# A perceiver block on one core: row statistics by group on GpSimd, one stream for two small attention layers, feed-forward and query projections interleaved

## The reference

```python
def _layernorm(x, axis=-1, eps=1e-05):
    m = jnp.mean(x, axis=axis, keepdims=True)
    v = jnp.var(x, axis=axis, keepdims=True)
    return (x - m) / jnp.sqrt(v + eps)
...
x = x + _L0_xattn_ref(_layernorm(x, axis=-1), ctx_1024, ctx_1024, ...)
x = x + _L0_attn_ref(_layernorm(x, axis=-1), ...)
x = x + _L0_ffn_ref(_layernorm(x, axis=-1), L0_ffn_weight, L0_ffn_weight_scale, L0_ffn_bias)
x = x + _L1_xattn_ref(_layernorm(x, axis=-1), ctx_1024, ctx_1024, mask_Bx1xSxS2_bf0, ...)
x = x + _L1_attn_ref(_layernorm(x, axis=-1), ...)
x = x + _L1_ffn_ref(_layernorm(x, axis=-1), ...)
```

## Time and profile before

| What | us |
|---|---|
| median of 3 runs (1117.49 to 1120.31) | 1117.58 |
| the profiled execution's own time | 1111.67 |
| its span | 1109.9 |
| busy: PE / DVE / ACT / POOL | 975.9 / 685.6 / 420.7 / 313.3 |
| first normalised tile | 24.64 |
| last tile of the second small layer normalised | 268.71 |
| first tile of the feed-forward normalised | 303.45 |
| first matmul of the cross attention's tiles | 378.03 |

### The profile page before, as it was taken

How to read it: one execution, slowest core, us unless ns; L and a number is a source line. 1 busy time by engine, 2 the same in 40 slices (tenths; PEclk the granted TensorE clock), 3 DMA queues, 4 the chain that set the end, 5 groups by cost and what they waited for, 6 DMA issues and landing times.

```text
span 1109.9 us, 40433 instructions
## 1 busy us (share of the span) xinstructions
PE 975.9 (88%) x16761; PEld 748.0 (67%) x16790; DVE 685.6 (62%) x1843; ACT 420.7 (38%) x1066; POOL 313.3 (28%) x328
## 2 busy tenths in 40 slices
PE   1899888998625899999999999999698979999999
PEld 0777656777412588888888888887477656666656
DVE  4678667887697366666666666666564633444436
ACT  1222223322253465655555565554433212222211
POOL 3101201110076234433333334431223024444430
PEclk9999888999856999999999999999697899999999
DMA  6000400000001011121111111110282011111116
GB/s 220 22 22 25 149 4 2 4 4 4 2 1 45 1 47 47 51 78 55 47 47 46 48 46 47 46 47 3 86 345 77 0 34 59 61 61 59 57 43 227
DMA packets 29743, 63.04 MB, mean 57 GB/s; under 512 B 5872, under 2 KB 22320, under 8 KB 26128
## 3 DMA queue, kind: packets, MB, share of 16 engines
q1 hardware_dynamic: 25840, 50.41, 13.0%
q0 software_dynamic: 3744, 10.23, 2.9%
HBM read 51.32 MB, written 9.31 MB: 55 GB/s over the span
## 4 chain that ended last, share of the span: by engine, by line
PE 57%; issue 5%; ACT 3%; DVE 3%; DVEq 0%; ACTq 0%; PEldq 0%
PE psum L722 13%; PE psum L1433 7%; PE psum L1441 6%; PE psum L795 6%; PE psum L784 4%; PE psum L810 3%; PE psum L1309 3%; ACT x_p L878 2%; PE psum L1088 2%; PE psum L1425 2%; PE psum L643 1%; PE psum L1329 1%; PE psum L765 1%; PE psum L1319 1%; PE psum L1194 1%
## 5 line engine op out<-in xcount | busy, mean ns | idle before, releaser
L878 ACT ACTIVATE x_p<-x_s,x_nmax 128x257 f32<-128x257 f32 x256 | 127.4, 499 | 112.0 <-DVE x_nmax L911 112.0
L941 DVE COPY x_pT<-psum 128x512 f32<-128x512 f32 x128 | 88.2, 689 | 67.7 <-PE psum L795 65.3
L911 DVE CUSTOM_DVE_ANT_0 x_s<-psum,x_mask 128x257 f32<-128x257 f32 x256 | 93.6, 423 | 44.3 <-PE psum L784 43.9
L795 PE MATMUL psum<-ident,x_p 128*128 128x128 f32 x512 | 80.0, 279 | 8.3 <-ACT x_p L878 1.7
L1433 PE MATMUL psum<-me_w,me_in 128*128 x156 | 77.1, 616 | 5.1 <-ACT me_in L1453 0.7
L1441 PEld LDWEIGHTS psum<-me_w,me_out 128*128 128x128 f32 x312 | 59.2, 190 | 25.3 <-issue 19.3
L1441 PE MATMUL psum<-me_w,me_out 128*128 x312 | 73.8, 379 | 0.9 <-DVE me_out L1488 0.9
L795 PEld LDWEIGHTS psum<-ident,x_p 128*128 128x128 f32 x512 | 58.2, 141 | 20.0 <-ACT x_p L878 18.3
L968 POOL TENSOR_TENSOR x_ctx1l<-x_ctx,x_ctx1h 128x2128 fp32r<-128x2128 f32 x8 | 37.9, 4743 | 113.6 <-ACT x_ctx1h L649 113.6
L1460 ACT ACTIVATE me_sh<-me_sb 128x512 f32<-128x512 f32 x39 | 24.5, 629 | 117.1 <-DVE me_sb L1474 117.1
L810 PEld LDWEIGHTS psum<-x_v,x_pT 128*32 128x32 f32 x4096 | 44.8, 112 | 32.8 <-DVE x_pT L941 20.1
(11 more groups left out here) (275 smaller groups left out, 2497.8 us busy)
## 6 DMA issues: line engine op xcount, KB each, us to landing
x_ctx<-in_ctx SPq DMA_DIRECT2D x16, 1064.0 KB, 4.9
me_w<-in_moe_w SPq DMA_DIRECT2D x8, 1024.0 KB, 12.4
me_got<-moe_outs SPq DMA_DIRECT2D x8, 512.0 KB, 8.2
x_mask<-in_mask SPq DMA_DIRECT2D x16, 128.5 KB, 3.7
x<-in_x SPq DMA_DIRECT2D x4, 512.0 KB, 5.5
sm_cT<-in_ctx SPq DMA_DIRECT2D x16, 128.0 KB, 2.1
me_eb<-in_moe_eb SPq DMA_DIRECT2D x1, 2048.0 KB, 24.6
moe_rows<-me_xn SPq DMA_DIRECT2D x4, 512.0 KB, 3.4
```

Source lines behind the costliest of these rows:

```text
L795: mm = nc.tensor.transpose(psum[:, 6, (2 * r + k) * P:(2 * r + k + 1) * P], x1_p[:, column(b, CB * c + r), k * P:(k + 1) * P], ident[:])
L878: nc.scalar.activation(x1_p[:, n, :], x1_s[:, rg, :], ACT.Exp, bias=x1_nmax[:, par, n:n + 1], scale=-1.0, accum_out=x1_sum[:, par, n:n + 1 ...
L911: nc.vector.tensor_tensor_reduce(out=x1_s[:, rg, :], in0=psum[:, 2 + rg, 0:SK], in1=x1_mask[par][:, b, :], scale=1.0, scalar=-2 * MASKED, ...
L941: nc.vector.tensor_copy(x1_pT[:, c].rearrange("p r k s -> p (r k s)"), psum[:, 6, :]).then_inc(x1["pT_ready"], 1)
```

## The change

Four things are changed. (1) For the first four layers the statistics are made per group of four tiles by GpSimd (`pool_rstd`: 15 operations of 128x4, one of them a power of -0.5, in 11 links that wait for one another), and no engine waits for more than its group (`group_ready`). The last two layers keep the old way. (2) The two small layers are one stream of 32 tiles; the bias product of the second layer is made in the fifth tile's last stages, its split bias after tile 8, the 8-bit weights at tile 15, the split weights of the cross attention after tile 20. (3) The feed-forward rounds and the query groups alternate: round i, then the queries of group i - 1, on TensorE and on ScalarE, which now normalises for the queries too and which takes turned tiles in pairs. (4) The first context is split after the last query normalisation, and GpSimd adds the cross attention's output bias to a tile of `x` within the tile loop.

```diff
+        layers = ["mix1", "moe1"]
+        early_layers = ["xattn0", "attn0", "ffn0", "xattn1"]
+        ln_ready, ln_step = sem("ln_ready"), sem("ln_step")
+        ln_work = sb("ln_work", [P, 6, U])
+        ln_power = sb("ln_power", [P, U])
+        ln_shift = sb("ln_shift", [P, NT])
+        ln_steps = [0]
+        ln_groups = [0]
+        def group_ready(eng, layer, g):
+            eng.wait_ge(ln_ready, early_layers.index(layer) * (NT // U) + g + 1)
+        def pool_rstd(pool, stats, count, g):
+            def done(*ins):
+                for i in ins:
+                    i.then_inc(ln_step, 1)
+                ln_steps[0] += len(ins)
+                pool.wait_ge(ln_step, ln_steps[0])
+            own = slice(g * U, (g + 1) * U)
+            mean, rstd = ln_mv[:, own, 0], ln_rstd[:, own]
+            diff, both, spread, var, root, power = (ln_work[:, n, :] for n in range(6))
+            pool.wait_ge(stats, count)
+            if ln_groups[0] > 0:
+                pool.wait_ge(ln_ready, ln_groups[0])
+            ln_groups[0] += 1
+            done(nc.gpsimd.tensor_tensor(diff, bn_out[:, own, 1], bn_out[:, own, 4], ALU.subtract),
+                 nc.gpsimd.tensor_tensor(both, bn_out[:, own, 1], bn_out[:, own, 4], ALU.add),
+                 nc.gpsimd.tensor_tensor(spread, bn_out[:, own, 2], bn_out[:, own, 5], ALU.add))
+            done(nc.gpsimd.tensor_scalar(mean, both, 0.5, None, ALU.mult),
+                 nc.gpsimd.tensor_tensor(diff, diff, diff, ALU.mult),
+                 nc.gpsimd.tensor_scalar(spread, spread, 1.0 / D, EPS, ALU.mult, ALU.add))
+            done(nc.gpsimd.tensor_scalar(diff, diff, 0.25, None, ALU.mult))
+            done(nc.gpsimd.tensor_tensor(var, spread, diff, ALU.add))
+            done(nc.gpsimd.tensor_tensor(root, var, ln_power[:], ALU.pow))
+            done(nc.gpsimd.tensor_tensor(power, root, root, ALU.mult))
+            done(nc.gpsimd.tensor_tensor(power, power, var, ALU.mult))
+            done(nc.gpsimd.tensor_scalar(power, power, -0.5, 1.5, ALU.mult, ALU.add))
+            done(nc.gpsimd.tensor_tensor(rstd, root, power, ALU.mult))
+            done(nc.gpsimd.tensor_tensor(both, mean, rstd, ALU.mult))
+            nc.gpsimd.tensor_scalar(ln_shift[:, own], both, -1.0, None, ALU.mult).then_inc(ln_ready, 1)
...
-            for s in range(NT + depth):
-                step(lambda d: (s - d, (s - d) % U), lambda d: 0 <= s - d < NT)
+            for s in range(len(smalls) * NT + depth):
+                step(lambda d: (s - d, (s - d) % U), lambda d: 0 <= s - d < len(smalls) * NT)
...
+                    if t == U:
+                        bias_product(smalls[1])
+                    if t in (0, U):
+                        pe.wait_ge(smalls[t // U].bias_ready, 1)
...
-            act_sqrt(act, c.name)
+        def small_scalar(act):
             nc.scalar.preload_act_table(ACT.Exp)
-            first = c.before
             act.wait_ge(sm_zeroed, 2)
-            act.wait_ge(sm["shift_ready"], smalls.index(c) + 1)
...
+                    if u == 0:
+                        group_ready(act, layer(t).name, t % NT // U)
+                    r = t % NT
+                    nc.scalar.activation(sm_xn[:, u, :], x[:, r, :], ACT.Identity, bias=ln_shift[:, r:r + 1],
+                                         scale=ln_rstd[:, r:r + 1]).then_inc(sm["norm_ready"], 1)
...
-            dve_rstd(dve, c.name)
-            nc.vector.scalar_tensor_tensor(out=sm_shift[:], in0=ln_mv[:, :, 0], scalar=-1.0, in1=ln_rstd[:], op0=ALU.mult,
-                                           op1=ALU.mult).then_inc(sm["shift_ready"], 1)
...
+                if live(0) and n(0)[0] == NT - 1:
+                    ffn_weights(dve)
...
+        def small_pool(pool):
+            for g in range(NT // U):
+                pool_rstd(pool, x_stats, U * (g + 1), g)
+                if g == 0:
+                    small_bias(pool, smalls[0])
+            for t in range(len(smalls) * NT):
+                r, c = t % NT, layer(t)
+                if r == 0:
+                    pool.wait_ge(c.bias_ready, 1)
+                pool.wait_ge(sm["norm_ready"], t + 1)
+                nc.gpsimd.tensor_tensor(x[:, r, :], x[:, r, :], c.b_o[:], ALU.add).then_inc(sm["x_biased"], 1)
+                if t == 8:
+                    small_bias(pool, smalls[1])
+                if t >= 10 and t % U == 2 and (t - 10) // U < NT // U + 2:
+                    g = (t - 10) // U
+                    pool_rstd(pool, sm["stats_ready"], U * (g + 1), g % (NT // U))
+                if t == 20:
+                    x1_pool_weights(pool)
...
+            dve.wait_ge(x1["weights_loaded"], 16 * 8)
+            dve.wait_ge(x1["bias_product"], 1)
+            nc.vector.tensor_tensor(x1_bo[:], psum[:, 6, 0:D], x1_bo[:], ALU.add).then_inc(x1["bias_ready"], 1)
...
+                if i == 0:
+                    pool_rstd(pool, sm["stats_ready"], NT + 3 * U, 2)
                 for u in range(U):
                     pool.wait_ge(f8["magic_ready"], U * i + u + 1)
                     v = f8_xn[:, i % 2, u, :]
                     nc.gpsimd.tensor_tensor(v, v, f8_magic[:, u, :], ALU.add).then_inc(f8["added"], 1)
+                if i == 0:
+                    pool_rstd(pool, sm["stats_ready"], NT + 4 * U, 3)
+                if i > 0:
+                    pool_rstd(pool, f8["stats_ready"], U * i, i - 1)
+            pool_rstd(pool, f8["stats_ready"], NT, ROUNDS - 1)
...
+                for v in range(PAIRS):
+                    act.wait_ge(f8["qT_done"], U * i + 2 * v + 2)
+                    if i > 0:
+                        act.wait_ge(f8["out_done"], U * (i - 1) + 2 * v + 2)
+                    nc.scalar.activation(f8_qT[:, 2 * v:2 * v + 2, :, :].rearrange("p u k s -> p (u k s)"),
+                                         psum[:, v, :].bitcast(BF16)[:, 0:2 * D], ACT.Copy).then_inc(f8["qT_ready"], 2)
+                if i > 0:
+                    queries_scalar(act, i - 1)
+            group_ready(act, "ffn0", ROUNDS - 1)
+            for k in range(KC):
+                context_high(act, 0, 0, k)
+            mask(act, 0, 0)
+            queries_scalar(act, ROUNDS - 1)
...
+        def queries_tensor(pe, i):
+            for v in range(PAIRS):
+                pe.wait_ge(x1["norm_ready"], U * i + 2 * v + 2)
+                if i > 0:
+                    pe.wait_ge(x1["xT_ready"], PAIRS * (i - 1) + v + 1)
+                for n in range(2):
                     for k in range(KC):
+                        mm = nc.tensor.transpose(psum[:, 4 + v, (n * KC + k) * P:(n * KC + k + 1) * P],
+                                                 x1_xn[:, 2 * v + n, k * P:(k + 1) * P], ident[:])
+                mm.then_inc(x1["xT_done"], 1)
+            pe.wait_ge(x1["xT_ready"], PAIRS * (i + 1))
+            if i == 0:
+                pe.wait_ge(x1["bias_ready"], 1)
+            for m in range(KC):
+                if i > 0:
+                    pe.wait_ge(x1["q_ready"], KC * (i - 1) + m + 1)
+                for k in range(KC):
+                    mm = nc.tensor.matmul(psum[:, 6 + m, :], x1_wq[:, k, m * P:(m + 1) * P], x1_xT[:, k, :],
+                                          start=(k == 0), stop=(k == KC - 1))
+                mm.then_inc(x1["q_done"], 1)
+        def queries_scalar(act, i):
+            group_ready(act, "xattn1", i)
+            if i > 0:
+                act.wait_ge(x1["xT_done"], PAIRS * i)
+            for u in range(U):
+                t = U * i + u
+                nc.scalar.activation(x1_xn[:, u, :], x[:, t, :], ACT.Identity, bias=ln_shift[:, t:t + 1],
+                                     scale=ln_rstd[:, t:t + 1]).then_inc(x1["norm_ready"], 1)
+            if i == 0:
+                group_ready(act, "ffn0", ROUNDS - 1)
+            else:
+                act.wait_ge(x1["q_done"], KC * i)
+            for v in range(PAIRS):
+                act.wait_ge(x1["xT_done"], PAIRS * i + v + 1)
+                nc.scalar.activation(x1_xT[:, :, v * 2 * P:(v + 1) * 2 * P].rearrange("p k (u s) -> p k u s", u=2),
+                                     psum[:, 4 + v, :].rearrange("p (u k s) -> p k u s", u=2, k=KC), ACT.Copy).then_inc(x1["xT_ready"], 1)
+            for m in range(KC):
+                act.wait_ge(x1["q_done"], KC * i + m + 1)
+                nc.scalar.activation(x1_qT[:, m, i * U * P:(i + 1) * U * P], psum[:, 6 + m, :], ACT.Identity,
+                                     bias=x1_bq[:, m:m + 1]).then_inc(x1["q_ready"], 1)
...
+            small_tensor(pe)
+            x1_bias_product(pe)
+            for i in range(ROUNDS):
+                ffn_tensor(pe, i)
+                if i > 0:
+                    queries_tensor(pe, i - 1)
+            queries_tensor(pe, ROUNDS - 1)
...
+            nc.gpsimd.memset(x1_plT[:], 0.0).then_inc(x1["zeroed"], 1)
+            pool.wait_ge(x1["bias_ready"], 1)
+            pool.wait_ge(x1["norm_ready"], NT)
+            x1_context(pool, 0, 0)
...
```

(2 more changed lines are left out.)

300 lines of the change are left out of this document (118 added, 182 removed).

## The result

The changed kernel took 1086.67 us (median of 4 runs, 1083.43 to 1088.43) against 1118.94 (1117.49 to 1121.35) of the kernel before, measured beside it: ratio 0.9706, 95% interval 0.9675 to 0.9737, 32.3 us less. Measured again it took 1087.74 against 1117.91, ratio 0.9742 (0.9696 to 0.9789), 30.2 less. The forecast was 22.8 less.

A forecast was written before the change was run, and what follows sets the result against it. TensorE was busy 88% of the span, with VectorE bounding the feed-forward. Start 7.7, boundary 13.2, feed-forward and queries 1.9 made 22.8 us less, taken from the median 1117.58: 1094.8 us, own range 1088 to 1101, 8 in 10 1083 to 1110.

The forecast's parts named there:

- Start: Up to the first normalisation: GpSimd's first group replaces the wait for VectorE's shift and 8-bit weights; 7.7 us less.
- R: Time of one group of statistics on GpSimd: 15 operations and 10 handovers, 4.2 us, between 2.5 and 17.7.
- Boundary: Between the two small layers: one stream removes 19.3 us of drain, statistics, table loads and refilling; 13.2 left after costs.
- The bias product: Second small layer's bias product: TensorE and VectorE wait for each other once; costs 1.9 us.
- Feed-forward and queries: From ScalarE free to the last query bias copy: alternating rounds and query groups gains 1.9 us.
- Second round, VectorE bound as today: Feed-forward's second round: VectorE still sets the pace, 8.3 us, ending at 320.4.
- the overlap wins only what ScalarE loses: Feed-forward and queries: what the overlap wins, ScalarE loses by waiting inside each query group; 1.9 us gained.
- Slopes of R: Loss per us of R: 1 at the start; in feed-forward and queries 1.3 under 5 us, 4.6 beyond.
- A: Rival, 20%: TensorE cold in every query group, projections 6.6 us instead of 4.6, 8 us more; 1102.8.
- B: Rival, 19%: TensorE warm, projections 3.70, no GpSimd interference, R = 3; 10 us less, 1084.6.
- C: Rival, 7%: GpSimd twice as slow, an operation 0.42 us, R 7.3; 14.7 us back, 1109.5.
- D: Rival, 8%: slower than before, the power a long routine; gain gone when R passes 8.7; about 1130 at R = 11.

The follow-up runs named there:

- e5: Changed kernel with VectorE making the 8-bit weights at the start, behind the first bias addition, instead of at tile 15: 1081.35 us, ratio to the kernel before 0.966.
- e2: Changed kernel with the two small layers again one after the other, a drain between them, statistics by group kept: 1101.47 us, ratio to the kernel before 0.9828.
- e1: Changed kernel with interleaving undone, the four feed-forward rounds first, then the four query groups: 1094.89 us, ratio to the kernel before 0.9792.
- e3: Changed kernel with four more, unused power operations in every group of statistics on GpSimd: 1114.35 us, ratio to the kernel before 0.9967.
- e4: Changed kernel without the four operations refining the power's result, so rows are less exact: 1079.88 us, ratio to the kernel before 0.9687.

## Why the prediction was right or wrong

**Direction and mechanism: right, but for what bounds the feed-forward; total: 22.8 forecast, 28.3 and 24.9 in the two profiles, 32.3 and 30.2 in the medians.**

- *Start.* 7.7 forecast, 7.81. R was 4.7, not 4.2: small operations and links as estimated, the power 1.05 instead of 0.21. The split bias was hidden, by 0.5 us.
- *Boundary, 13.2 forecast, 15.9 (second profile 14.6).* Against the 15.9 stand three costs that I put at 6.1. The weights: 2.7 forecast as nothing hidden, 1.5 by e5; TensorE had work queued (7.05 us busy in the 7.47 step), so the rotation was late only in the next step. The bias product: 1.9 forecast; the two steps around it take 9.87 and 6.08, 2.2 more than two of 6.89. GpSimd beside VectorE: 1.5 forecast, nothing seen; TensorE bounds this stream (62.5 of 65.4 us busy in the earlier trace rows), and a VectorE operation twice as long has slack. So this term was mis-sized by the bound that I took for it: VectorE's, where it is TensorE's. Together they cost 3.7 instead of 6.1, which would have made 19.3 - 3.7 = 15.6. That this is nearly the 15.9 measured is in part luck: some 2 us of the 15.9 are the clock's (below), so that about as much cost stands in this part that I can name no place for. e2 shows that it was mostly the drain that cost, not the statistics: 14.8 us came back in the medians.
- *Drain.* I counted nothing; from the last normalisation to ScalarE's last copy it took 29.4 before and 26.9 after (27.7 in the second profile, 26.7 to 28.3 in the variants), with the same instructions. Some 2 us of gain that no step foresaw. The clock is not the cause, the granted one was 0.88 and 0.87; In the kernel before TensorE stood still for 1.78 us ahead of 275.11, where it waited for nothing, and in the changed kernel's drain the longest such standstill is 0.31. So 1.5 of the 2.4 us are luck of that execution; the rest stays open.
- *Feed-forward and queries, 1.9 forecast, 2.2 (second profile 4.1).* The sum came out because errors cancelled; a step in it did not. "Second round, VectorE bound as today" is wrong: GpSimd bounds it, by the chain and by e1. The first query group began 28.3 us after ScalarE was free, not 26.1, and ended at 39.2, not 36.2; the second took 8.1 us instead of 10.1, and that won most of it back. From there the times fell as forecast: VectorE idle 11.67 (9), group ends 53.3, 64.2 and 77.4 us after ScalarE was free (52.3, 64.3, 77.6), ScalarE waiting for TensorE in each. Projections 5.24 on average (second profile 4.76) against 4.6. The judgement that the overlap wins only what ScalarE loses was wrong as a statement on the edit: without it the stretch is 8 us longer (e1). The feed-forward's 47.42 us there are 10 more than the earlier trace rows's 37.55, but 5.4 of these are statistics that stood ahead of it before; from ScalarE's last copy on it is 47.3 against 42.9, 4.4 us more by the statistics on GpSimd. The interleaving pays for them, and more.
- *Slopes of R.* For the 4.3 us of e3 they give 23.1; the profile has 24.3 without the projections, the medians 27.7. Below 4.7 us it is 3.5 per us in e4's profile instead of 2.3: the bend at 5 us may have been reached already, since a group that takes 4.7 at the start takes over 5 beside VectorE.
- *Rivals.* A (cold projections, 6.6 each) came in part: 6.29, 3.70, 5.25, 5.73. B's time (1084.6) was the nearest, for other reasons: in the first profile only one projection took 3.70, and R was 4.7, not 3. C and D fell with R = 4.7.
- *Median against profile.* I carried a difference within one profiled execution to the median. That execution, 1111.67, was one of the luckier: 31 runs of the kernel before lay between 1109.34 and 1124.4. The changed kernel's, 1083.43, was the fastest of its eight (to 1092.68), so the 28.3 compare two lucky ones.
- *The printed clock of the start.* The bias product rested on 2.04 us "at the low clock", while the earlier trace rows prints a granted clock of 1.00 there. Four matmuls of that size took 1.03 us at a granted clock of 1.00 and 1.91 at 0.50 later (last section), so the duration speaks for the low level, and against the clock printed there.

## What to carry to other kernels

When an edit moves work to an idle engine, write down that engine's pace per round afterwards (here 2.7 + 3.1 + 5.4 us) and compare it with the bound before costing anything else: it became the bound although over the whole span it is busy 28% before and 35% after. In a pipeline bound by TensorE, as this one, work added to another engine's queue costs only what exceeds the slack of a step, while a drain costs its length and a low clock in the refilling. Independent work of an in-order engine belongs between its request to another engine and its wait for the answer.
